# Perceiver layer on one core: the host lays out transposed inputs, the prologue covers one quarter of x, and the expert loop is written out

## What is computed

```python
def reference(x, ctx, ...):
    x = x + xattn(layernorm(x), ctx, Wq, Wk, Wv, Wo, bo)    # 16 heads of 64
    x = x + rwkv(layernorm(x), mix_k, mix_v, mix_r, W_key, W_value, W_rec, W_out, decay, first)
    x = x + ffn(layernorm(x), Wr, br, W1, b1, W2, b2)
    return x

def xattn(x, context, Wq, Wk, Wv, Wo, bo):
    dots = einsum('bhnd,bhmd->bhnm', heads(x @ Wq), heads(context @ Wk)) * 64 ** -0.5
    return merge(softmax(dots) @ heads(context @ Wv)) @ Wo + bo

def rwkv(x, ...):
    x_prev = pad(x)[:, :-1]                                  # one token back
    k = (x * mix_k + x_prev * (1 - mix_k)) @ W_key.T         # v and r likewise, r through a sigmoid
    ...                                                      # decayed cumulative sums of exp(k) * v and exp(k) over time
    return (r * num / den) @ W_output.T

def ffn(x, Wr, br, W1, b1, W2, b2):                          # 8 experts, 512 wide
    expert = argmax(x @ Wr.T + br)                           # one expert for each token
    return (relu(x @ W1[expert].T + b1[expert]) @ W2[expert].T + b2[expert])
```

## Time and profile before

| | us |
|---|---|
| runs | 1046.47, 1040.83, 1046.96; median 1046.47 |
| profiled execution | 1041.88, its span 1039.8 |
| mean granted clock of PE over the span | 0.936 of full |
| PE busy | 908.2 (87% of the span) |
| DVE busy | 809.0 (78%) |
| ACT busy | 712.0 (68%) |
| POOL busy | 700.8 (67%) |

### The profile page before, as it was taken

How to read it: one execution, slowest core, us unless ns; L and a number is a source line. 1 busy time by engine, 2 the same in 40 slices (tenths; PEclk the granted TensorE clock), 3 DMA queues, 4 the chain that set the end, 5 groups by cost and what they waited for, 6 DMA issues and landing times.

```text
span 1039.8 us, 31371 instructions
## 1 busy us (share of the span) xinstructions
PE 908.2 (87%) x9098; PEld 764.9 (74%) x9099; DVE 809.0 (78%) x2325; ACT 712.0 (68%) x2040; POOL 700.8 (67%) x1210
## 2 busy tenths in 40 slices
PE   3799999999999999999999999999998374078885
PEld 3678888888888888888888888888886273056664
...
DMA packets 46505, 32.35 MB, mean 31 GB/s; under 512 B 6518, under 2 KB 44065, under 8 KB 46448
## 3 DMA queue, kind: packets, MB, share of 16 engines
...
...
## 4 chain that ended last, share of the span: by engine, by line
PE 38%; POOL 31%; issue 17%; ACT 5%; DVE 4%; POOLq 1%; DMA 1%; ACTq 1%; SPq 1%; DVEq 0%
POOL Pn L774 13%; PE bank L388 6%; PE bank L411 6%; PE bank L433 4%; PE bank L1299 4%; PE bank L400 3%; POOL chi L756 3%; PE bank L426 3%; PE bank L1314 2%; POOL sorted_rows L1103 2%; ACT Pe L560 2%; POOL sraw L856 2%; POOL cT L766 2%; POOL e12p L781 1%; ACT hr L1189 1%
## 5 line engine op out<-in xcount | busy, mean ns | idle before, releaser
L774 POOL TENSOR_TENSOR Pn<-Pe,rsum 128x1028 f32<-128x1028 f32 x128 | 243.0, 1899 | 132.1 <-DVE rsum L644 132.1
L560 ACT ACTIVATE Pe<-bank,nmax 128x257 f32<-128x257 f32 x512 | 242.9, 480 | 17.4 <-DVE nmax L630 11.0
L630 DVE TENSOR_REDUCE nmax<-bank 128x1 f32<-128x257 f32 x512 | 203.4, 418 | 42.2 <-PE bank L388 38.9
L388 PE MATMUL bank<-cT,qh 96*128 96x257 f16 x1024 | 185.3, 275 | 9.4 <-issue 3.9
L552 ACT ACTIVATE Th<-bank 128x512 f16<-128x512 f32 x256 | 141.4, 595 | 49.9 <-PE bank L433 49.9
L624 DVE TENSOR_TENSOR Tl<-bank,Th 128x512 f16<-128x512 f32 x256 | 174.3, 682 | 0.5 <-ACT Th L552 0.4
L433 PE MATMUL bank<-identf,Pn 128*128 128x128 f32 x1024 | 147.0, 273 | 0.0
L388 PE MATMUL bank<-cT,ql 96*128 96x257 f16 x512 | 139.5, 272 | 0.0
L433 PEld LDWEIGHTS bank<-identf,Pn 128*128 128x128 f32 x1024 | 114.7, 142 | 5.6
L388 PEld LDWEIGHTS bank<-cT,qh 96*128 96x128 f16 x1024 | 93.7, 98 | 21.5 <-issue 9.5
L560 ACT ACTIVATION_READ_ACCUMULATOR Pe<-bank,nmax 128x1 f32 x512 | 107.3, 210 | 0.0
...
## 6 DMA issues: line engine op xcount, KB each, us to landing
...
Z<-last_rows SPq DMA_DIRECT2D x128, 2.2 KB
...
out_dram<-yout,idx POOLq DMA_INDIRECT x40, 2.3
```

Source lines behind the costliest of these rows:

```text
L388: last = nc.tensor.matmul(bank[SB[t]][:, 0:M], w[:, par, b, t * P:(t + 1) * P], cT[:, s4, c, 0:M], start=(k == 0), stop=(k == 2))
L560: nc.scalar.activation(Pe[:, n_par(j + 1), t, :], bank[SB[t]][:, 0:M], ACT.Exp, bias=nmax[:, n_par(j + 1), t:t + 1], accum_out=sums[:, n_p ...
L630: nc.vector.tensor_reduce(nmax[:, n_par(j + 1), t:t + 1], bank[SB[t]][:, 0:M], AX.X, ALU.max, negate=True).then_inc(s_nmax, 1)
L774: nc.gpsimd.tensor_tensor(Pn[:, par, :, :], Pe[:, par, :, :], rsum[:, par, :].unsqueeze(2).broadcast_to([P, QT, M]), ALU.mult)\
```

## The change

The host hands over Wq, Wk, Wv, the four mix weights, Wr, W1, W2, b1 and the mix vectors transposed, and, as a new input beside ctx, `ctxT`, the whole context with channels first (96 x 257 per sequence). In the kernel:

1. `load_ctx` gets a second DMA, of `rawT` (four sequences, 96 x 257 fp32 each). `pe_ctxT` is gone. `act_cT` copies `rawT` to the high part of `cT` for n+4, instead of both parts for n+2 from bank 7; POOL's `pool_cT` subtracts for the low part (`TENSOR_TENSOR` 96x257, L916) where `pool_last` stood.
2. The prologue takes statistics of x's first quarter only, `rstd` on POOL (`pool_rstd1`) instead of ACT and DVE, the four groups of A products, one unit, and four q projections from that unit. The B products go to steps -1 to 2, seven units (normalize, transpose, split) to steps 4, 6, 8, 10, 12, 14 and 20, the statistics of the other quarters to steps 0, 1, 4, 6, 8 and 10, their rstd to 2, 6 and 10, the mix tables to 3, 5 and 7, and the additions of `bo` to the units' steps.
3. W1 and W2 are split from SBUF, with no transposition, and their 16 DMAs become 8.
4. `over_tiles` has no hardware loop; one `value_load` serves eight tiles.

```diff
-        def pe_ctxT(n, s8, s4):
-            wait(nc.tensor, s_clo, n + 1)
-            wait(nc.tensor, s_cT, n)
-            wait(nc.tensor, s_L12, n - 2)
-            for half, src in enumerate((chi, clo)):
-                for c in range(MC):
-                    last = nc.tensor.transpose(bankh[7][0:CC, (half * MC + c) * P:(half * MC + c + 1) * P],
-                                               src[:, s8, c, :], ident[:, :])
-            last.then_inc(s_ctxT, 1)
...
             pe_mix(it, j, n)
+            pe_early(n)
...
+        UNIT = {4: 1, 6: 2, 8: 3, 10: 4, 12: 5, 14: 6, 20: 7}
+
+        def pe_early(n):
+            n = n_static(n)
+            if n is not None and -1 <= n < 3:
+                k = n + 1
+                wait(nc.tensor, s_ql, n + 6)
+                wait(nc.tensor, s_wvo, 32)
+                for a in range(4):
+                    lo, pair = (k % 2) * D, k // 2 * 4 + a
+                    last = nc.tensor.matmul(bank[3][0:CC, a * C:(a + 1) * C], wvT[lo:lo + D, pair, :],
+                                            wo_r[lo:lo + D, pair, :], start=True, stop=True)
+                last.then_inc(s_ab, 1)
+            if n in UNIT:
+                wait(nc.tensor, s_ql, n + 6)
+                wait(nc.tensor, s_xn1, UNIT[n] + 1)
+                pe_norm_T(UNIT[n] % 2, 3, s_x1T)
...
+        def dve_early(n):
+            n = n_static(n)
+            if n in (0, 1):
+                dve_moments1(range(GQ + CT * n, GQ + CT * n + CT))
+            if n in (4, 6):
+                dve_moments1(range(2 * GQ + CT * (n - 4) // 2, 2 * GQ + CT * (n - 4) // 2 + CT))
+            if n in (8, 10):
+                dve_moments1(range(3 * GQ + CT * (n - 8) // 2, 3 * GQ + CT * (n - 8) // 2 + CT))
+            if n is not None and n + 1 in UNIT:
+                dve_norm1(UNIT[n + 1])
...
+        def dve_early_end(n):
+            n = n_static(n)
+            if n is not None and -1 <= n < 3:
+                k = n + 1
+                wait(nc.vector, s_abh, 5 + k)
+                nc.vector.tensor_tensor(heads(Blo, k), bank[3][0:CC, :].rearrange("p (a c) -> p a c", a=4),
+                                        heads(Bhi, k), ALU.subtract).then_inc(s_abl, 1)
+            if n in UNIT:
+                dve_x1l(UNIT[n])
...
-        def act_cT(n, s4):
-            wait(nc.scalar, s_ctxT, n + 1)
-            nc.scalar.activation(cT[:, s4, :, 0:MC * P], bankh[7][0:CC, 0:2 * MC * P].rearrange("p (s m) -> p s m", s=2),
-                                 ACT.Copy).then_inc(s_cT, 1)
+        def act_cT(n, s4, par, b):
+            wait(nc.scalar, s_S, QT * (n - 3))
+            nc.scalar.activation(cT[:, s4, 0, 0:M], rawT[:, par, b, :], ACT.Copy).then_inc(s_cTh, 1)
...
-        def pool_last(n, s4):
-
-            wait(nc.gpsimd, s_S, QT * (n - 3))
-            nc.gpsimd.tensor_copy(cT[:, s4, :, MC * P:M], c256T[:, :, bass.ds(n, 1)]).then_inc(s_lcol, 1)
+        def pool_cT(n, s4, par, b):
+
+            wait(nc.gpsimd, s_cTh, n + 1)
+            nc.gpsimd.tensor_tensor(cT[:, s4, 1, 0:M], rawT[:, par, b, :], cT[:, s4, 0, 0:M], ALU.subtract)\
+                .then_inc(s_cT, 1)
...
-                pack = eng.value_load(pk[0:1, bass.ds(it, 1)], min_val=0, max_val=E ** NV - 1) if routed else None
+            packs, experts = {}, {}
+
+            def expert(s):
+                q, digit = divmod(s, PK)
+                if q not in packs:
+                    packs[q] = eng.value_load(pk[0:1, q:q + 1], min_val=0, max_val=E ** PK - 1)
+                if s not in experts:
+                    experts[s] = (packs[q] // E ** digit) % E
+                return experts[s]
+
+            for it in range(NT // UN + 2):
                 for u in range(1 - UN, 1):
-                    step(it, u, lambda v: (pack // E ** (v + 5)) % E)
-            for it in range(3):
-                block(it)
-            with eng.Fori(3, NT // UN) as it:
-                block(it)
-            for it in range(NT // UN, NK):
-                block(it)
...
                 wait(sp, s_clo, GB * (g - 1))
+                wait(sp, s_cT, GB * (g - 1))
+                sp.dma_start(rawT[:, par, :, :], ctxT[bass.ds(b0, GB), :, :].rearrange("b c m -> c b m"))\
+                    .then_inc(s_ctxT[par], 16)
...
-            for k in range(6):
-                src, w = ((wq_r, P), (wk_r, CC), (wv_r, CC))[k // 2]
+            for k in range(4):
...
+            for c in range(GB):
+                pe_q(c, c, slice(0, P), QB[c], 0)
             pipeline(nc.tensor, pe_step)
...
-                nc.vector.tensor_tensor(lo[:, k // 2, :], bank[4 + k % 4][:, :], hi[:, k // 2, :], ALU.subtract)\
+                src = (w1r, w2fr)[k % 2]
+                nc.vector.tensor_tensor(lo[:, k // 2, :], src[:, k // 2, :], hi[:, k // 2, :], ALU.subtract)\
```

521 lines of the change are left out of this document (263 added, 258 removed).

## The result

The changed kernel takes 1033.01 us (median of 6 runs, 1030.91 to 1034.44), the kernel before 1043.86 (6 runs, 1040.83 to 1048.10): ratio 0.9892, with a 95% interval of 0.9861 to 0.9923. The forecast was 1016 us, in a range of 993 to 1033. So the sign is right, but the gain, 10.9 us, is less than half of the forecast one (28), and the time lies just past the top of the range. The profiled execution took 1033.19 us, its span is 1031.2 (before: 1041.88 and 1039.8).

What follows compares the result with a forecast made beforehand. It took waits to bound the prologue, PE the plateau, with a loop through DVE and POOL behind it. 1041.9 - 26.1 + 9.5 - 2.6 - 0.3 (drain) - 8.5 = 1013.9, plus half the distance between run levels: 1016 us, range 993 to 1033.

Steps and rivals of the forecast that it cites:

- Prologue: Before the first score: first score at 25.3 us instead of 51.44, -26.1 us, bounds -20 to -27.
- the two levels of the kernel before: Whole kernel: runs at 1040.83 and about 1046.47 us; half the distance was added to 1013.9, giving 1016.
- Early steps, "back in: +9.5": Work moved into early steps: +8 us in steps 0 to 15, +1.5 for unit n=20; bounds +2.5 to +20.8.
- Loop, "-2.6": Main loop: period of 8 steps from 46.97 to 46.80 us, 13 times, -2.6 us.
- first leg: Loop period, PE's j=4 start through DVE and POOL to PE taking xn: from 22.66 to 23.37 us.
- Expert loop, "-8.5": Expert loop written out, eight tiles to a load: -8.5 us, bounds -13 to 0.
- second leg: Loop period, PE alone from taking xn to the next j=4: from 24.31 to 23.43 us.
- Scatter, "nothing": Ahead of the expert loop: weight split moved off PE beside POOL's 32 indirect DMAs, which set the end; no change.
- More goes back in: Rival: early steps in series (+20.8 us) or POOL's new operation stretched to 1.05 us (loop +9.6); 1027 to 1028; chance 0.20.
- The transpositions come back whole: Rival in the loop: L510's wait does not bind, so the loop gives 23.1 us instead of 2.6; 995 us; chance 0.20.
- Writing out brings nothing: Rival in the expert loop: the 0.82 us is load and experts' arithmetic, not the branch; 1024.5 us; chance 0.10.
- POOL becomes the bound: Rival in the loop: POOL's new operation at 1.33 us or more eats the gain; at 1.5, 1064 us; chance 0.04.

Runs made afterwards that it cites:

- e1: The kernel before with only the expert loop (`over_tiles`) written out, eight tiles to a load: 1031.26 us, ratio 0.9883.
- e13: The changed kernel with POOL's seven deferred additions of `bo` over 8 of 128 columns (computation partly left out): 1028.18 us, ratio 0.9857.
- e3: The changed kernel with POOL's subtraction for the low part of `cT` over 2 of 257 columns (computation partly left out): 1013.25 us, ratio 0.9726.
- e8: The changed kernel without DVE's 24 deferred statistics, the first quarter's values used instead: 1033.37 us, ratio 0.988.
- e9: The changed kernel with 14 extra identity transpositions on PE in each of two gaps ahead of and in step -1: 1032.52 us, ratio 0.9882.
- e6: The changed kernel with the four groups of B products and their splits ahead of the pipeline, not in steps -1 to 2: 1029.04 us, ratio 0.9852.
- e2: The changed kernel with POOL's `cT` subtraction replaced by one of two columns plus two write-only memsets, POOL occupied as long: 1035.34 us, ratio 0.9931.
- e15: The kernel before with one extra POOL subtraction 96x257 per step, result unused, transpositions kept: 1073.89 us, ratio 1.0265.
- e4: The changed kernel with POOL doing `xd` and `xn` at j=6 before the context splits and `cT`: 1016.86 us, ratio 0.9742.
- e5: The kernel before with POOL doing `xd` and `xn` at j=6 before the context splits: 1037.15 us, ratio 0.991.

## Why the prediction was right in part and wrong in the main

**Prologue: right, with two terms off that offset each other in part.** -28.0 against -26.1, the first score at 23.41 against 25.3. DVE's statistics and the weights' transpositions are gone from it as worked out, and its first product starts at 8.53 (forecast 8.4).

```profile
8.53 4.89 PE L1313 MATMUL bank<-wkT,wqT 64*128 64x96 f32 x32 [8.53 <-DMA wqT<-in_dram]
...
11.25 2.66 POOL L1192 MEMSET Z<- 128x3072 f16 x1
...
11.55 3.00 DVE L525 TENSOR_SCALAR xn<-R,mv,rst 128x128 f32<-128x128 f32 x4
```

The A products took 4.89 us instead of 7.8. The sum had no wait for the normalized unit: PE waits 1.20 us for `xn`, whose four normalizations took 3.00 us beside a memset of POOL's that stood elsewhere before, against 1.11. To the forecast of the whole I also added half the distance between the two levels of the kernel before, 2.3 us. The changed kernel has no such levels (1030.9 to 1034.4), and the two sorts of prologue under e1 are the likely source of them, which wasn't tried.

**Early steps, "back in: +9.5": the step that failed most.** +22.2 to step 16 and +5.2 behind it, above even the upper bound of 20.8. The sum had PE and DVE in it and left out POOL, the engine that each step's `Pn` waits for. The prediction put POOL's part at nothing, without a reason. Three rstd chains of 3.2 us (one operation 1.66 at 78.89), six additions of 1.17 and the tables come to some 18 us there, and the new `cT` in 16 steps to another 7 (16 x (0.60 - 0.14)). e13, e3 and e8 show POOL to be the bound of steps 4 to 15. The prologue's POOL work had been free, because PE and DVE set its end; moved into steps, it was not. The second part is steps 0 to 3, +11.5 us: the low clock up to 4 (e9), the B products about 4 (e6), and the rest not told apart. The forecast saw half clock for the first scores only. Of the +5.2 in steps 16 to 31, the cT operation accounts for all (e3: 93.57, against 93.77 before). One such place is a wait of 2.70 us of L656 at 180.41, behind which the granted clock is 0.66 for 5 us (180.22 to 185.22).

**Loop, "-2.6": the mechanism right, the first leg mis-sized.** The two legs, the wait at L656 (1.46 against 1.7), the operation's size (0.685 busy, about 0.60 from start to start, as forecast) and the place where the transpositions' time went all came as worked out. The term that failed is DVE's part of the first leg, put at -0.2: `rsum` of j=5 came 0.40 later. In e3, where the subtraction is short, it comes 0.13 earlier, so the -0.2 itself was about right, and what the sum lacked is +0.54 for the hold-up: POOL's longer occupation holds up DVE's operations on SBUF (a scan of 1.3 us, `num` at 940), and through them `rsum`. The other term, +0.92 for POOL's part, was 0.30 too large, since POOL had lost time beside DVE before the change too (`xn` at 1.06). The two misses partly cancel. I had the Trainium skill's rule, "SBUF — State Buffer", "Who interferes with whom", and looked only for POOL as the one that waits, as in xn's 1.06; here DVE waits too, and POOL's `xn` got faster. The sum for the leg was 23.37, measured 23.77; that is most of the miss, and the second leg adds 0.18. The same section of the Trainium skill also says that VectorE's two-input operations meet only those of GpSimd that read SBUF. The trace of e2 doesn't agree: a scan lasted 1.22 us, through two memsets and the operation behind them. e15 shows the operation alone to lengthen the first leg.

**Expert loop, "-8.5": right in kind, too small.** -12.7 (e1: -11.4). The mean distance of `hr` fell from 109.49 / 39 = 2.81 to 96.76 / 39 = 2.48. My own figure for the eleven boundaries was 13.3; the 4.8 that I took off again for four loads and register work didn't show in it; 1.0 of them may be what came ahead of the first `hr` (see the scatter).

**Scatter, "nothing": wrong by 2.1,** of which 1.9 are the issue of four indirect DMAs beside DVE's splits, one source of which had been in PSUM before. It wasn't tried by an experiment; the two rows stand beside each other in time and no more is shown.

**The rivals.** "More goes back in" (1027 to 1028, 0.20) was the case nearest to what came, with the engines exchanged: POOL was the one with too much work in the early steps, and DVE the one held up in the loop (DVE's own wait for POOL was not in it). Its two forms came together, the first at +27.4, the second at +3.95 instead of +9.6; larger gains elsewhere kept the total from going further up. "The transpositions come back whole" fell: e4, with the wait for `xn` gone from its list of waits, gained 0.99 a period and then stood where e5 stands, which still has them. "Writing out brings nothing" is refuted by e1. "POOL becomes the bound" from 1.33 us an operation on didn't come to that in the loop, but in steps 4 to 15 POOL is the bound at 0.66.
